# Cumulative sums and convolution taps read from PSUM, norm deviations on ScalarE

## The reference

```
x = x + mamba(norm(x))      # H: in-projection, 4-tap causal convolution, silu,
                            #    softplus dt, recurrence over 512 channels x 16 states, gate, out-projection
x = x + ffn(norm(x))        # F: down(silu(gate) * up), 768 wide
x = x + wkv(norm(x))        # K: receptance, key, value of 1024 channels:
    e  = exp(clip(-w*(T-t) + K)),  eu = exp(clip(U + K))
    A  = shift(cumsum(e * V)) + eu * V
    B  = shift(cumsum(e)) + eu
    out = (sigmoid(R) * A / B) @ Wo
x = x + ffn(norm(x))        # R: the same ffn again
norm(x) = (x - mean) / sqrt(var + 1e-5)
```

## Time and profile before

| | |
|---|---|
| Median of 3 runs | 1877.59 us |
| The profiled execution | 1873.11 us |
| Its span | 1871.3 us |
| DVE busy | 1646.3 us, 88%, 2109 instructions |
| PE busy | 1489.6 us, 80%, 4800 |
| POOL busy | 1389.5 us, 74%, 1035 |
| ACT busy | 1178.2 us, 63%, 1705 |
| ACT table loads | 191 by `need`, 1283 ns each |
| Mean granted PE clock | 0.904 |

### The profile page before, as it was taken

One profiled execution on the slowest core, in us unless ns is written; L12 is line 12 of the kernel. 1 busy time (PEld: TensorE's weight loads), 2 busy tenths in 40 slices (PEclk: granted clock), 3 DMA queues, 4 the chain that ended last, 5 costly groups with the idle time before them and its releaser, 6 DMA issues. The chain is left out here.

```text
span 1871.3 us, 18954 instructions
## 1 busy us (share of the span) xinstructions
PE 1489.6 (80%) x4800; PEld 720.6 (39%) x4800; DVE 1646.3 (88%) x2109; ACT 1178.2 (63%) x1705; POOL 1389.5 (74%) x1035
## 2 busy tenths in 40 slices
PE   4262358778879888989979798988989697988987
PEld 1120113333435335443535345443635253445454
DVE  3299899999999989999999999999999999994571
ACT  3674457676658765877567575876677356743621
POOL 0669997986997698886987679886988876761340
PEclk8685669899989889999989899999999898999999
DMA  7533434522434432452334434362335222211210
GB/s 230 213 120 107 157 118 154 188 94 92 146 101 160 149 121 90 128 190 96 117 115 156 137 96 137 118 211 87 113 109 172 90 80 94 94 55 49 62 40 29
DMA packets 167614, 225.20 MB, mean 120 GB/s; under 512 B 13457, under 2 KB 104082, under 8 KB 167506
## 3 DMA queue, kind: packets, MB, share of 16 engines
q1 hardware_dynamic: 167506, 223.99, 36.8%
HBM read 179.90 MB, written 39.85 MB: 117 GB/s over the span
## 5 line engine op out<-in xcount | busy, mean ns | idle before, releaser
L932 POOL TENSOR_TENSOR bu<-rep,bc 128x512 f32<-128x512 f32 x512 | 696.3, 1383 | 107.0 <-PE ps_y L1435 102.2
L1248 DVE TENSOR_TENSOR_SCAN ps_d<-ps_d,bu 128x512 f32<-128x512 f32 x384 | 458.1, 1212 | 59.7 <-POOL bu L932 50.3
L1076 ACT ACTIVATE ps_d<-rep,scale_a 128x512 f32<-128x512 f32 x512 | 337.9, 683 | 209.9 <-DVE bu L1255 186.6
L1384 PE MATMUL ps_r<-xT,wgu 128*128 128x512 f32 x768 | 360.0, 611 | 25.1 <-ACT kv L1113 6.6
L975 ACT ACT_TABLE_LOAD x191 | 245.1, 1283 | 76.5 <-PE ps_r L1384 29.7
L1384 PE MATMUL ps_r<-mix,wkv 128*128 128x512 f32 x512 | 254.4, 640 | 40.3 <-DVE mix L1316 16.2
L1255 DVE TENSOR_TENSOR bu<-ps_d,bc 128x512 f32<-128x512 f32 x384 | 252.3, 674 | 0.5
L1435 PE MATMUL ps_y<-bu,sel 128*32 128x512 f32 x1024 | 156.3, 686 | 118.9 <-DVE bu L1255 78.5
L1384 PEld LDWEIGHTS ps_r<-xT,wgu 128*128 128x128 f32 x768 | 144.2, 194 | 229.3 <-issue 220.5
L937 POOL TENSOR_TENSOR bu<-bu,bc 128x512 f32<-128x512 f32 x128 | 174.9, 1367 | 49.4 <-DVE bu L1248 48.8
L949 POOL TENSOR_TENSOR kv<-sums,kv 128x1024 f32<-128x1024 f32 x64 | 150.8, 2357 | 77.4 <-DVE sums L1345 45.3
(11 more groups left out here) (98 smaller groups left out, 2077.8 us busy)
## 6 DMA issues: line engine op xcount, KB each, us to landing
rep<-dd_scratch SPq DMA_DIRECT2D x128, 512.0 KB, 4.6
wgu<-gu_scratch SPq DMA_DIRECT2D x96, 256.0 KB, 2.7
bc<-bc_scratch SPq DMA_DIRECT2D x64, 256.0 KB, 3.6
dd_scratch<-xs SPq DMA_DIRECT2D x32, 512.0 KB, 3.4
wo<-w_o_dram SPq DMA_DIRECT2D x16, 512.0 KB, 3.9
win<-w_in_dram SPq DMA_DIRECT2D x64, 128.0 KB, 2.2
wr<-w_r_dram SPq DMA_DIRECT2D x64, 128.0 KB, 2.6
wkv<-w_k_dram SPq DMA_DIRECT2D x64, 128.0 KB, 2.3
```

What stands on the lines that cost most here:

```text
L932: pool.tensor_tensor(bu[:, i % BU, :], rep[:, g % REP, 1, :], bc[:, 0, q, :], ALU.mult)\
L1076: act.activation(ps_d[D_BANK[i]][:, :], rep[:, g % REP, 0, :], ACT.Exp, scale=scale_a[:, a, NQ * j + q:NQ * j + q + 1]).then_inc(decay_rea ...
L1248: dve.tensor_tensor_scan(states, d[:, :], bu[:, i % BU, :], 0.0, ALU.mult, ALU.add)\
L1384: last = pe.matmul(dst, lhs, rhs, start=n == 0, stop=n == len(pairs) - 1)
```

## The change

Four edits are made together, and the tables `ORDER` and `BANKS` are written anew for all engines.

1. The taps read the PSUM bank of `p_in` itself. ACT computes the tap of the current token over the whole tile from PSUM, DVE adds the three older tokens, each over 512 minus its distance. The copy to `xs` is gone; dt has a tile `dd` of its own. The bank is released by the last tap.
2. `v_ev` is two instructions: `eu*V` to SBUF, and `e*V` back into the PSUM bank of V. The second sum reads it there, beside the ones in SBUF. The bank of V is released by the second sum.
3. The first sum is a scan with add and bypass: it adds `e` to its state and has the same PSUM bank as an operand that it does not use.
4. ACT computes the deviation of the norms as exp(-0.5·ln(var + eps)), the negated mean and the shift, in five small instructions (`ha_std`, `fa_std`, `ra_std`). DVE's lines 1188 and 1195 and POOL's 898 are gone.

```diff
@@ norm, on ACT (new; gone: variance and shifts on DVE, norm on POOL)
+            def deviation(f, seq, i):
+                part = slice(2 * (i % 2), 2 * (i % 2) + 2)
+                act.wait_ge(n_moments[f].sem, at(n_moments[f], seq, 2 * (i + 1)))
+                need("natural_log_exp_and_others")
+                act.activation(rstd[f][:, part], moments[f][:, part, 1], ACT.Ln, bias=eps[:, 0:1]).then_inc(n_log[f].sem, 1)
+                act.activation(minus_mean[f][:, part], moments[f][:, part, 0], ACT.Identity, scale=-1.0)\
+                    .then_inc(n_rstd[f].sem, 1)
+                act.wait_ge(n_log[f].sem, at(n_log[f], seq, i + 1))
+                act.activation(rstd[f][:, part], rstd[f][:, part], ACT.Exp, scale=-0.5).then_inc(n_rstd[f].sem, 1)
+                act.wait_ge(n_rstd[f].sem, at(n_rstd[f], seq, 2 * i + 2))
+                for t in range(2 * (i % 2), 2 * (i % 2) + 2):
+                    last = act.activation(shift[f][:, t:t + 1], minus_mean[f][:, t:t + 1], ACT.Identity,
+                                          scale=rstd[f][:, t:t + 1])
+                last.then_inc(n_shift[f].sem, 1)
@@ released
-                "p_in": (xs_ready, i + 1) if i < JD ...
+                "p_in": (conv_tap, TAP_DONE[TAPS * i + TAPS - 1]) if i < JD ...
-                "p_v": (ev_ready, i + 1)
+                "p_v": (ev_summed, i + 1)
@@ a_in, a_tap
-                            act.copy(xs[:, i, TAPS - 1:], src[:, :]).then_inc(xs_ready.sem, 1)
...
-                        act.activation(xc[:, i, :], xs[:, i, 0:T], ACT.Identity, bias=col("conv_b", i),
-                                       scale=col("conv_w", TAPS * i)).then_inc(first_tap.sem, 1)
+                        act.activation(xc[:, i, :], src[:, :], ACT.Identity, bias=col("conv_b", i),
+                                       scale=col("conv_w", TAPS * i + TAPS - 1)).then_inc(first_tap.sem, 1)
@@ v_tap
-                        dve.scalar_tensor_tensor(xc[:, j, :], xs[:, j, tap:tap + T], col("conv_w", i), xc[:, j, :],
+                        dve.scalar_tensor_tensor(xc[:, j, back:], src[:, 0:T - back],
+                                                 col("conv_w", TAPS * j + TAPS - 1 - back), xc[:, j, back:],
                                                  ALU.mult, ALU.add).then_inc(conv_tap.sem, 1)
@@ v_ev
-                        dve.scalar_tensor_tensor(rows(i, "ev", "euv"), src[:, :].unsqueeze(1).to_broadcast([P, 2, T]),
-                                                 col("bv", i), rows(i, "e", "eu"), ALU.add, ALU.mult)\
-                            .then_inc(ev_ready.sem, 1)
+                        dve.scalar_tensor_tensor(kv[:, row(i, "euv"), :], src[:, :], col("bv", i), kv[:, row(i, "eu"), :],
+                                                 ALU.add, ALU.mult).then_inc(ev_ready.sem, 1)
+                        dve.scalar_tensor_tensor(src[:, :], src[:, :], col("bv", i), kv[:, row(i, "e"), :],
+                                                 ALU.add, ALU.mult).then_inc(ev_ready.sem, 1)
@@ v_esum, v_evsum
-                        dve.tensor_tensor_scan(sums[:, 0, 1:], ones[:, 0:1].to_broadcast([P, T]), kv[:, row(i, "e"), :], 0.0,
-                                               ALU.mult, ALU.add).then_inc(e_summed.sem, 1)
+                        dve.wait_ge(ev_ready.sem, at(ev_ready, r, 2 * i + 2))
+                        unused = ps_r[BANK[r, "p_v", i]]
+                        dve.tensor_tensor_scan(sums[:, 0, 1:], kv[:, row(i, "e"), :], unused[:, :], 0.0,
+                                               ALU.add, ALU.bypass).then_inc(e_summed.sem, 1)
...
-                        dve.tensor_tensor_scan(sums[:, 1, 1:], ones[:, 0:1].to_broadcast([P, T]), kv[:, row(i, "ev"), :], 0.0,
-                                               ALU.mult, ALU.add).then_inc(ev_summed.sem, 1)
+                        dve.tensor_tensor_scan(sums[:, 1, 1:], ones[:, 0:1].to_broadcast([P, T]),
+                                               ps_r[BANK[r, "p_v", i]][:, :], 0.0, ALU.mult, ALU.add).then_inc(ev_summed.sem, 1)
@@ ORDER, the first words for ACT
-        "ha_norm*2 ha_turn*2 a_in a_tap a_in a_tap a_xc*2 a_in a_tap a_in a_tap a_xc*2 a_xproj ..."
+        "ha_std*2 ha_norm*2 ha_turn*2 a_tap*2 a_xc*2 a_tap*2 a_xc*2 a_xproj ..."
```

More of the change, by code:

```diff
@@ L101 @@
     "p": (
[L102 to L115, removed]
-        "p_wo2 p_wo p_wo2 p_y fp_turn fp_turn2 fp_turn fp_turn2 rp_turn p_k p_v p_recept rp_turn2 p_y rp_turn "
@@ L543, in hybrid_block @@
         ones = sb("ones", [P, P])
[L544 removed]
+        eps = sb("eps", [P, 1])
         xin = sb("xin", [P, TT, C])
@@ L1007, in run @@
                     elif unit == "a_in":
-                        src = full(m_full, m, "p_in", i)
-                        if i < JD:
-                            prev = before(m)
-                            if i == 0 and prev is not None:
-                                for k in range(2):
-                                    act.wait_ge(dd_stored[k].sem, at(dd_stored[k], prev, dd_stored[k].per))
-                            act.copy(xs[:, i, TAPS - 1:], src[:, :]).then_inc(xs_ready.sem, 1)
-                        else:
-                            j = i - JD
-                            if j >= 2:
-                                act.wait_ge(sz_stored[j % 2].sem, at(sz_stored[j % 2], m, 16))
-                            need("silu_and_others")
-                            act.activation(sz[:, j % 2, :], src[:, :], ACT.Silu).then_inc(sz_ready.sem, 1)
+                        src, j = full(m_full, m, "p_in", i), i - JD
+                        if j >= 2:
+                            act.wait_ge(sz_stored[j % 2].sem, at(sz_stored[j % 2], m, 16))
+                        need("silu_and_others")
+                        act.activation(sz[:, j % 2, :], src[:, :], ACT.Silu).then_inc(sz_ready.sem, 1)
                     elif unit == "a_tap":
@@ L1042, in run @@
                         dt, dtx = dd_slot(i)[:, 0, :], dd_slot(i)[:, 1, :]
+                        prev = before(m)
                         if i >= 2:
                             act.wait_ge(dd_stored[i % 2].sem, at(dd_stored[i % 2], m, 16))
+                        elif prev is not None:
+                            act.wait_ge(dd_stored[i % 2].sem, at(dd_stored[i % 2], prev, dd_stored[i % 2].per))
                         act.activation(dtx, src[:, :], ACT.Abs, bias=bias).then_inc(sp_abs.sem, 1)
@@ L1230, in run @@
                         aggregate("h", t, i)
-                    elif unit == "hv_eps":
-                        variance("h", t, i)
-                    elif unit == "hv_shift":
-                        shifts("h", m, i)
                     elif unit == "v_tap":
-                        j, tap = i // TAPS, i % TAPS
-                        if tap == 1:
+                        j, back = i // TAPS, i % TAPS
+                        src = ps_r[BANK[m, "p_in", j]]
+                        if back == 1:
                             dve.wait_ge(first_tap.sem, at(first_tap, m, j + 1))
```

617 lines of the change are left out of this document (294 added, 323 removed), and 117 rows, old and new, of tables (BANKS, ORDER).

## The result

The changed kernel takes 1823.1 us in the median (1817.5 to 1827.7, 4 runs), the one before 1877.6 (1875.4 to 1877.7, 4 runs). The ratio is 0.9711, 95% interval 0.9677 to 0.9745: 54.5 us faster, of 95.6 forecast. The profiled execution took 1817.51 us, its span is 1815.7.

The account below looks back on a forecast made before the run. DVE was taken to bound the kernel, busy 96.2% between first and last scan of the recurrence. Head 78, that stretch 1465 and tail 233 make 1776 us; with 1.8 and 4.5 us added, 1782 us, range 1743 to 1842.

Parts of the forecast that it names:

- DVE's work: DVE busy time between first and last scan of the recurrence: 1496.3 us less 116.5 plus 5, giving 1384.8 us.
- the body: Stretch in which all 512 scans of the recurrence run: 1555.7 us before, forecast 1465 us.
- The norms: Lines 1195 and 1188 vanish from DVE between first and last scan: 45.0 us less, bounds 40 to 54.
- chain: Five small ACT instructions per norm deviation: 1.2 us each, 64 of them, 77 us in all.
- I take a DVE share of 94.5%: DVE's busy share between first and last scan, lowered from 96.2% for PE and bank holds: 1465 us instead of 1439.
- PE takes over: Rival: longer bank holds keep PE to 83.5% between first and last scan, DVE idles: 1827 us, chance 0.17.
- The signs of being wrong: Sums staying at 1.6 us; DVE below 92%, PE waiting for taps or sums; scans awaiting ACT's decays by tens of microseconds.
- ACT is hidden: ACT's added work, to some 1252 us or 70%, costs no time; uncovered, at most 77 + 15 us.
- Sums that stay slow: Rival: the attention's scans on DVE gain nothing from their new forms, 42 us stay: 1827 us, chance 0.08.
- everything fits: Rival: DVE keeps its steady 96.9% between first and last scan, 1429 us there: 1741 us total, chance 0.10.
- slower: Rival: 291 us of longer PSUM bank holds delay PE; gain gone above 40%, 1907 us at 50%; chance 0.08.

Follow-up runs that it names:

- a dose of 243 us: Changed kernel with V's banks freed only after POOL's add that follows the second sum, lengthening 64 holds in all by this amount: 1868.9 us, ratio 0.9958.

## Why the prediction was right and wrong

- **Which way, and through what.** Right. The mechanism on DVE, an instruction with two SBUF operands that waits for POOL and one with a PSUM operand that doesn't, is shown by the single lines after, and by the two experiments that put one operand back into SBUF. The trace before says the same: of its 224 taps and sums, 129 began while a POOL instruction was running; its rest was 0.65 to 0.94 us in the mean of the three lines, and they took 0.60 to 0.80 us more than the fastest. None of the other 95 was over 0.15 us slow.
- **DVE's work.** Forecast 1384.8 us in the body, measured 1391.1. Taps 94.0 to 59.3, as forecast (35.4); first sum 18.4 for 50 (forecast 18.2), second 24.6 (23.8). The norms were mis-sized: 45.0 forecast, 34.7 where they were changed alone. POOL's durations fell as expected, 1383 to 1293 for its largest group. ACT: 1.25 us for 1.2 per chain, 68% for 70%.
- **The step that failed** is "I take a DVE share of 94.5%", 26 us for all banks and PE. Measured 92.3%: 1391.1 / 0.923 is 1507 us, where 1391.1 / 0.945 would be 1472. These 35 us, and the 6 of DVE's work, are the 41. The step let DVE's idle time in the body grow from 59 us to 80; it grew to 116, by 37 us in waits for PE and 16 in waits for ACT. The body's own share of 96.2% was read as if time followed work. The experiments show that in this kernel, in a fixed order, time follows 0.3 to 0.5 of what is taken off DVE (0.16 for the norms alone, 38.7 us of work in all for 6) and 0.7 to 0.8 of what is added. The whole change, with an order made for it, got 54.5 for 122.3 us less of DVE in all (1646.3 to 1524.0), 0.45.
- **Rival: PE takes over.** Its numbers fit (83.5% and 1827 against 83.0% and 1823), better than the forecast's, and so does the side on which DVE idles, waiting for PE. Bank holds can be dear, as the longer hold of V shows. That PE's amount of work is the bound isn't borne out, since 384 matmuls less gave nothing; that its speed is on the path is not excluded, by the clocks above.
- **The signs of being wrong.** DVE below 92% with PE waiting for taps or sums nearly came: 92.3%, and 36 us of such waits. Scans wait 19.2 us for ACT's decays in the body, 12.1 before, so not by tens more.
- **ACT is hidden.** Wrong by some 11 us, give or take 7: without the chains the changed kernel is that much faster.
- **Rivals that fell.** Sums that stay slow, everything fits, slower. The last put the added hold at 291 us, where the trace has 786, and its break-even at 40% of it. In a fixed order a dose of 243 us cost 0.19 per us; in an order made for them the 786 cost 0.09 at most, if all of the 26 us allowed and the 41 missing were theirs. The taps' holds showed no price.
- **Open.** How the 41 us divide. DVE's order holds 16 to 21, the chains some 11; these may overlap. What the change's own longer hold of V's banks costs was not measured: the product would need rows of SBUF that the changed kernel doesn't have, so an early release wasn't tried. By the 0.19 of the one dose its 316 us would be an estimate of 60 us, nearly all of those 26 and 41; but that price was taken in a fixed order, and PE itself waits less for these banks than before. What the granted clock does to the time, and what the time does to it, is open. Whether the orders of PE and ACT hold more is open as well.

## What to carry to other kernels

A high busy share on one engine does not make its work the price of time: where all engines run in fixed orders, take the worth of a microsecond from an experiment (one edit alone, or a little work left out) before multiplying. An edit that changes many durations needs its order made again, and the order tried on its own afterwards, since here a tenth of DVE's places was worth a third of the whole gain. A PSUM operand spares a VectorE instruction the wait for GpSimd even when it is not used, but price the bank's hold, read from a trace and not from the durations of its readers: 3.8 us more on 64 of them cost 46.
